# Routed experts: Gelu outputs in pairs of chunks, a lead of four chunks, and a tile's high token part on ScalarE

## The chip, the cores and the metric

The program runs on one core of one Trainium2 chip. The metric is the device time of one execution in microseconds, the median of several. The program has two parts that follow each other: an attention-like part with the shared experts (about 900 us), and the routed experts (about 510 us). Only the second is changed.

## The reference, cut to what matters

```
x = x + mlstm_cell(layernorm(x), ctx, ctx, ...)        # first part, unchanged
u = layernorm(x)
h_s = shared experts of u                              # first part, unchanged
scores = sigmoid(u @ centroids); gpk, i_topk = top_k(scores, 2); gk = gpk / scores.sum(-1)
xn = u * rsqrt(mean(u * u) + eps) * g_routed
h  = gelu(einsum('btc,ech->bteh', xn, W1_r) + b1_r)    # C 256, H 1024, 8 experts
routed = einsum('bteh,ehc->btec', h, W2_r) + b2_r
out = x + u + h_s + sum over the two chosen experts of gk * routed
```

## The kernel before, in words

The first part writes each token twice, once for each chosen expert, into a DRAM buffer sorted by expert (8 x 512 tokens, two experts each). The second part (`stage_c`, from L1034) walks over NT = 39 tiles of T = 256 sorted tokens, each with one expert. n is the tile, i = n % 2 its buffer, r = n // 2.

**Two-part products.** Each float32 factor is used as a high part (rounded to fp32r, a cast) and a low part (the factor minus its high part). A product is three matmuls: high x high, high x low, low x high. So each tile's tokens need xhi and xlo, its weights whi and wlo, and the Gelu outputs hhi and hlo.

**Tile n on TensorE** (`body`, L1141). Before the first matmul it waits for xhi, for xlo and for the first NP1 = 4 of the tile's wlo pieces (L1144 to L1146), which hold all of W1. Then it goes through M = 8 chunks m of 128 hidden units: the up-product of chunk m (six matmuls of 256 columns, L1155) into one of NU = 4 banks, and after it the second product of the chunk that lies LAG = 2 earlier (`second`, six matmuls, L1135), for m < LAG that of the tile before. Behind the up-product of chunk XSTEP = 3 come four transposes of the next tile's tokens (L1119). In the text, U3 is the moment at which the up-product of chunk 3 has been issued, U7 the same for chunk 7.

**ScalarE** (`body`, L1196), in program order for each m: Gelu of chunk m from the bank into hraw (L1206), the cast into hhi (L1209); at m = LAG the scaled output yt of the tile before (`output`, L1186, two instructions L1192); then one piece of whi (L1184, `weights`).

**VectorE** (`body`, L1264), in program order for each m: wait for hhi of the chunk, hlo = hraw - hhi (L1273), then one piece of wlo (L1233); at m = XSTEP, ahead of the piece, xT (`tokens`, L1236: two scalings out of the banks, L1242), at m = M - 2 xlo (`tokens_low`, L1247), and behind m = M - 1 four very small instructions that find the tokens' owners (`owners`).

**Which piece of weights a step makes** is decided by `piece_of` (L1079), for ScalarE and VectorE alike:

```
def piece_of(m):
    return (m - LAG) % M, m >= LAG
```

The weights of a tile are 8 pieces of 128 x 512 (4 of W1, then 4 of W2). With LAG = 2, chunks 2 to 7 of tile n make pieces 0 to 5 of tile n + 1, and chunks 0 and 1 of the next tile the pieces 6 and 7. Pieces 3 and 7 (BY_POOL, L1077) are not cast by ScalarE but by GpSimd.

**GpSimd** (`body`, L1317), in program order for each tile: the cast of piece 3 of the next tile (L1297) once the second products of the tile before are done, two indirect DMAs that add yt into the output (`add_up`, L1313) once yt is made, the cast xhi of the next tile's tokens (L1304) once xT is made, the cast of piece 7.

**SyncE** issues the loads of tile n (tokens, W1, W2, bias) once wlo of tile n - 2 is complete (L1096).

The Gelu buffers hraw, hhi and hlo have NHB = 4 slots of one chunk each.

Of the kernel before, what the change touches and what calls it, by code (L numbers as in the profile page):

```python
# [4 lines left out]
fp32 = mybir.dt.float32  # L5
# [14 lines left out]
def xattn_moe_kernel(nc, x, ctxt, ig_w, ig_b, fg_w, fg_b, ln_scale, g_s, W1_s, b1_s, W2_s, b2_s,  # L20
# [9 lines left out]
    M = HID // P  # L30
# [29 lines left out]
    with whole:  # L60
# [972 lines left out]


        stage_c = ExitStack()
        NHB = 4
        Cc = lambda name, shape, dt=fp32: sb(stage_c, name, shape, dt)
        PIECE = 2 * WN // M
        NP1 = WN // PIECE
# [45 lines left out]
        with nc.Block() as block:  # L1085
# [25 lines left out]
            @block.tensor  # L1111
            def _(pe):
                def transposes(n, i, r):
                    pe.wait_ge(t_x[i], 16 * r + 16)
                    if n > 0:
                        pe.wait_ge(t_xraw, n)
                    for k in range(KD):
                        for j in range(TJ):
                            last = nc.tensor.transpose(x_bank[k][:, j * P:(j + 1) * P], xt[i][:, j, 2 + k * P:2 + (k + 1) * P],  # L1119
                                                       ident[:, :])  # L1120
                    last.then_inc(t_tr, 1)

                def second(n, i, m):

                    pe.wait_ge(t_hhi, M * n + m + 1)
                    pe.wait_ge(t_hlo, M * n + m + 1)
                    if m % 2 == 0:
                        pe.wait_ge(t_wlo, M * n + NP1 + m // 2 + 1)
                    if m == 0 and n > 1:
                        pe.wait_ge(t_y, n - 1)  # L1130
                    h = m % NHB
                    wsl = slice(WN + m * D, WN + (m + 1) * D)
                    for j in range(TJ):
                        for t, (l, w) in enumerate(((hhi, whi), (hhi, wlo), (hlo, whi))):
                            last = nc.tensor.matmul(  # L1135
                                y_bank[i][j * D // 512][:, (j * D) % 512:(j * D) % 512 + D], l[:, h, j * P:(j + 1) * P],
                                w[i][:, wsl], start=m == 0 and t == 0 and (j * D) % 512 == 0,
                                stop=m == M - 1 and t == 2, skip_group_check=True)
                    last.then_inc(t_step, 1)

                def body(n, i, r):  # L1141
                    if n == 0:
                        transposes(0, 0, 0)
                    pe.wait_ge(t_xhi, n + 1)  # L1144
                    pe.wait_ge(t_xlo, n + 1)
                    pe.wait_ge(t_wlo, M * n + NP1)  # L1146
                    for m in range(M):

                        if not (n == 0 and m < NU):
                            pe.wait_ge(t_gelu, M * n + m - NU + 1)  # L1150
                        ub = psum[m % NU]
                        for k in range(KD):
                            wsl = slice(k * HID + m * P, k * HID + (m + 1) * P)
                            for t, (w, x_) in enumerate(((whi, xhi), (whi, xlo), (wlo, xhi))):
                                last = nc.tensor.matmul(ub[:, 0:T], w[i][:, wsl], x_[i][:, k, :],  # L1155
                                                        start=k == 0 and t == 0, stop=k == KD - 1 and t == 2)
                        last.then_inc(t_up, 1)
                        if m == XSTEP and n < NT - 1:
                            transposes(n + 1, 1 - i, r + i)
                        if m >= LAG:  # L1160
                            second(n, i, m - LAG)
                        elif n > 0:
                            second(n - 1, 1 - i, M - LAG + m)
                    if n == NT - 1:
                        for m in range(M - LAG, M):
                            second(n, i, m)
                for n in range(NT):
                    body(n, n % 2, n // 2)

            @block.scalar  # L1170
            def _(sc):
                def weights(n, i, r, m):

                    if m == 0:
                        sc.wait_ge(t_w1[i], 16 * r + 16)
                    if m == NP1:
                        sc.wait_ge(t_w2[i], 16 * r + 16)
                    if n > 1 and m == 0:

                        sc.wait_ge(t_step, M * (n - 1))  # L1180
                    if m in BY_POOL:
                        return
                    psl = slice(m * PIECE, (m + 1) * PIECE)
                    nc.scalar.copy(whi[i][:, psl], raw[i][:, psl]).then_inc(t_whi, 1)  # L1184

                def output(n, i, r):  # L1186
                    sc.wait_ge(t_step, M * n + M)
                    sc.wait_ge(t_meta, n + 1)
                    if n > 1:
                        sc.wait_ge(t_acc, 16 * TJ * (n - 1))  # L1190
                    for j in range(TJ):
                        last = nc.scalar.activation(yt[i][:, j, :], y_bank[i][j * D // 512][:, (j * D) % 512:(j * D) % 512 + D],  # L1192
                                                    ACT.Copy, scale=gate[n % NG][:, j:j + 1])
                    last.then_inc(t_y, 1)

                def body(n, i, r):  # L1196
                    if n == 0:
                        for m in range(M - LAG):
                            weights(0, 0, 0, m)
                    sc.wait_ge(t_b1[i], 16 * r + 16)  # L1200
                    for m in range(M):
                        sc.wait_ge(t_up, M * n + m + 1)
                        if not (n == 0 and m < NHB):

                            sc.wait_ge(t_step, M * n + m - NHB + 1)
                        nc.scalar.activation(hraw[:, m % NHB, :], psum[m % NU][:, 0:T], ACT.Gelu,  # L1206
                                             bias=b1[i][:, m:m + 1]).then_inc(t_gelu, 1)
                        sc.wait_ge(t_gelu, M * n + m + 1)
                        nc.scalar.copy(hhi[:, m % NHB, :], hraw[:, m % NHB, :]).then_inc(t_hhi, 1)  # L1209
                        if m == LAG and n > 0:  # L1210
                            output(n - 1, 1 - i, r - 1 + i)
                        piece, ahead = piece_of(m)
                        if not ahead:
                            weights(n, i, r, piece)
                        elif n < NT - 1:
                            weights(n + 1, 1 - i, r + i, piece)
                    if n == NT - 1:
                        output(n, i, r)
                for n in range(NT):
                    body(n, n % 2, n // 2)  # L1220

            @block.vector
            def _(dve):
# [40 lines left out]
                def body(n, i, r):  # L1264
# [4 lines left out]
                            weights(0, 0, m)  # L1269
                        owners(0, 0)  # L1270
                    for m in range(M):
                        dve.wait_ge(t_hhi, M * n + m + 1)
                        nc.vector.tensor_tensor(hlo[:, m % NHB, :], hraw[:, m % NHB, :],  # L1273
                                                hhi[:, m % NHB, :].bitcast(fp32), ALU.subtract).then_inc(t_hlo, 1)
                        piece, ahead = piece_of(m)
                        if not ahead:
                            weights(n, i, piece)
                        elif n < NT - 1:
                            if m == XSTEP:
                                tokens(n + 1, 1 - i)  # L1280
                            if m == M - 2:
                                tokens_low(n + 1, 1 - i)
                            weights(n + 1, 1 - i, piece)
                            if m == M - 1:
                                owners(n + 1, 1 - i)
                for n in range(NT):
# [3 lines left out]
            def _(pool):  # L1290
# [5 lines left out]
                    psl = slice(m * PIECE, (m + 1) * PIECE)  # L1296
                    nc.gpsimd.tensor_copy(whi[i][:, psl], raw[i][:, psl]).then_inc(t_wpool, 1)  # L1297

                def tokens(n, i):

                    if n > 1:
                        pool.wait_ge(t_up, M * (n - 1))
                    pool.wait_ge(t_xraw, n + 1)
                    nc.gpsimd.tensor_copy(xhi[i][:, :, :], xT[:, :, :]).then_inc(t_xhi, 1)  # L1304

                def add_up(n, i):

                    pool.wait_ge(t_y, n + 1)
# [7 lines left out]

                def body(n, i, r):  # L1317
                    if n == 0:
                        tokens(0, 0)
                        weights(0, 0, 0, BY_POOL[0])  # L1320
                        weights(0, 0, 0, BY_POOL[1])
                    if n < NT - 1:
# [1 line left out]
                    if n > 0:  # L1324
                        add_up(n - 1, 1 - i)
                    if n < NT - 1:
                        tokens(n + 1, 1 - i)
                        weights(n + 1, 1 - i, r + i, BY_POOL[1])
                    else:
                        add_up(n, i)  # L1330
# [28 lines left out]
```

## Time and profile before

| | |
|---|---|
| median of 3 executions | 1432.65 us (1430.29 to 1432.75) |
| the profiled execution, its own time | 1436.01 us |
| its span | 1434.3 us |
| mean granted TensorE clock over the span | 0.951 |
| routed experts, first to last TensorE matmul | 917.3 to about 1424 us |
| TensorE busy in the span | 1170.9 us (82%) |
| VectorE busy | 1026.1 us (72%) |
| ScalarE busy | 793.5 us (55%) |
| GpSimd busy | 389.5 us (27%) |

A row of the timeline gives the start in us from the span's start, the duration in us, the engine (PE is TensorE, DVE VectorE, ACT ScalarE, POOL GpSimd), the line of the kernel, the operation, output and inputs, the shape, how many instructions were merged, and in brackets the idle time of the engine just before with what ended it; "issue" means that the profile shows no releaser. A duration holds some 0.1 us in which the engine already starts its next instruction, so the distance between two starts is the better price of one of several in a row. Matmuls overlap even more: a duration of 0.28 us at a distance of 0.12 us.

### The profile page before, as it was taken

The numbers are of one execution on the slowest core, as the hardware profiler recorded it, in microseconds if no ns is written. First come the engines' busy times: TensorE is split into PE (matmuls) and PEld (weight loads), VectorE is DVE, ScalarE is ACT, GpSimd is POOL, SyncE is SP. The second block draws the span as 40 slices with busy tenths as digits, with TensorE's granted clock in tenths as the row PEclk, the third lists the DMA queues.
The fourth block names the chain that finished last, engine by engine and source line by source line (L and its number), as shares of the span: only waits on it lengthen the run. The fifth ranks groups of instructions, "written<-read, shape, count | busy, mean of one in ns | idle before, by whom it ended". The sixth has DMA issues, their size and how long they took to land. (4 is left out here: it accounts for less than half of the span.)

```text
span 1434.3 us, 22326 instructions
## 1 busy us (share of the span) xinstructions
PE 1170.9 (82%) x7861; PEld 1008.2 (70%) x7861; DVE 1026.1 (72%) x2507; ACT 793.5 (55%) x1454; POOL 389.5 (27%) x397
## 2 busy tenths in 40 slices
PE   0363698797897987997978988599999999999996
PEld 0142477576676666775766777589888999899886
DVE  2356659568567676595684654588898889888984
ACT  2101355444553554554544443488888887888785
POOL 2312122041041121221410201144334433443343
PEclk9986799999999999999999998799999999999998
DMA  4899910000010010000000000677777777777772
GB/s 125 220 265 273 288 61 30 30 30 30 30 59 30 20 41 30 30 31 30 30 15 15 31 19 27 213 206 194 194 218 210 198 190 214 216 198 194 205 220 24
DMA packets 172563, 168.08 MB, mean 117 GB/s; under 512 B 48362, under 2 KB 159860, under 8 KB 172452
## 3 DMA queue, kind: packets, MB, share of 16 engines
q1 hardware_dynamic: 120884, 109.43, 25.3%
q10 hardware_dynamic: 37264, 38.54, 10.5%
q0 software_dynamic: 14304, 18.69, 6.3%
q8 instruction: 63, 1.03, 0.3%
q14 instruction: 48, 0.39, 0.1%
HBM read 109.42 MB, written 57.22 MB: 116 GB/s over the span
## 5 line engine op out<-in xcount | busy, mean ns | idle before, releaser
L1233 DVE TENSOR_TENSOR wlo<-raw,whi 128x512 fp32r<-128x512 f32 x312 | 228.2, 732 | 35.1 <-ACT whi L1184 31.4
L1155 PE MATMUL bank<-xhi,whi 128*128 128x256 f32 x624 | 178.8, 287 | 25.5 <-issue 20.2
L1206 ACT ACTIVATE hraw<-bank,b 128x256 f32<-128x256 f32 x312 | 148.2, 475 | 86.2 <-PE bank L1155 53.1
L1273 DVE TENSOR_TENSOR hlo<-hraw,hhi 128x256 fp32r<-128x256 f32 x312 | 183.1, 587 | 17.5 <-ACT hhi L1209 5.7
L973 PE MATMUL bank<-whs,shared_hhi 128*128 128x256 f32 x512 | 150.0, 293 | 50.1 <-DVE shared_hlo L727 50.1
L1135 PE MATMUL bank<-whi,hhi 128*128 128x256 f32 x624 | 180.3, 289 | 12.8 <-issue 11.4
L523 ACT ACTIVATE shared_hraw<-bank,b1s 128x512 f32<-128x512 f32 x128 | 88.1, 688 | 180.8 <-PE bank L988 171.4
L1155 PE MATMUL bank<-xlo,whi 128*128 128x256 f32 x624 | 175.3, 281 | 0.0
L1155 PE MATMUL bank<-xhi,wlo 128*128 128x256 f32 x624 | 175.1, 281 | 0.0
L1135 PE MATMUL bank<-whi,hlo 128*128 128x256 f32 x624 | 173.4, 278 | 0.0
L1135 PE MATMUL bank<-wlo,hhi 128*128 128x256 f32 x624 | 173.3, 278 | 0.0
L727 DVE TENSOR_TENSOR shared_hlo<-shared_hraw,shared_hhi 128x512 fp32r<-128x512 f32 x128 | 89.9, 706 | 114.1 <-ACT shared_hhi L526 107.5
L458 POOL DMA_INDIRECT sorted_tokens<-rowbuf,slots x64 | 66.3, 1036 | 371.9 <-DVEq L808 354.8
L1184 ACT CAST whi<-raw 128x512 fp32r<-128x512 f32 x234 | 143.9, 616 | 17.3 <-DMA raw<-in_L_ffn_W_r_dram 17.3
L1313 POOL DMA_INDIRECT out_dram<-yt,token x78 | 121.3, 1556 | 96.1 <-ACT yt L1192 84.2
L973 PE MATMUL bank<-wls,shared_hhi 128*128 128x256 f32 x512 | 146.8, 287 | 0.0
L973 PE MATMUL bank<-whs,shared_hlo 128*128 128x256 f32 x512 | 146.5, 286 | 0.0
L973 PEld LDWEIGHTS bank<-whs,shared_hhi 128*128 128x128 f32 x512 | 100.0, 195 | 63.5 <-DVE shared_hlo L727 59.3
L1155 PEld LDWEIGHTS bank<-xhi,whi 128*128 128x128 f32 x624 | 118.4, 190 | 32.5 <-issue 32.5
L1297 POOL CAST whi<-raw 128x512 fp32r<-128x512 f32 x78 | 79.2, 1016 | 213.3 <-PE bank L1135 207.1
L1209 ACT CAST hhi<-hraw 128x256 fp32r<-128x256 f32 x312 | 126.8, 406 | 9.9
L988 PE MATMUL bank<-xhs,whs 128*128 128x512 f32 x256 | 117.4, 459 | 17.0 <-DVE xls L746 11.8
(248 smaller groups left out, 2834.7 us busy)
## 6 DMA issues: line engine op xcount, KB each, us to landing
raw<-in_L_ffn_W_r_dram SPq DMA_DIRECT2D x78, 1024.0 KB, 7.8
sorted_tokens<-base ACTq DMA_DIRECT2D x1, 33540.0 KB, 137.6
xt<-sorted_tokens SPq DMA_DIRECT2D x39, 260.0 KB
big<-in_L_ffn_W_s_dram SPq DMA_DIRECT2D x4, 1024.0 KB
xb<-in_x_dram SPq DMA_DIRECT2D x8, 512.0 KB, 4.6
cb<-in_ctx_dram SPq DMA_DIRECT2D x8, 512.0 KB, 3.6
xr<-in_x_dram SPq DMA_DIRECT2D x8, 512.0 KB, 3.6
out_dram<-base ACTq DMA_DIRECT2D x8, 512.0 KB, 2.9
```

What stands on the lines that cost most here:

```text
L523: nc.scalar.activation(hraw[:, k % NHB, :], up_bank[k % 2][:, :], ACT.Gelu, bias=b1s[:, k // M, k % M:k % M + 1]).then_inc(gelu_done, 1)
L727: tt(hlo[:, k % NHB, :], hraw[:, k % NHB, :], hhi[:, k % NHB, :].bitcast(fp32), ALU.subtract).then_inc(hlo_ready, 1)
L973: last = mm(down_bank[j // 2][:, (j % 2) * D:(j % 2 + 1) * D], h[:, k % NHB, j * P:(j + 1) * P], w[:, e, wsl], start=k == 0 and t == 0 and ...
L988: last = mm(up_bank[k % 2][:, :], w[:, e, wsl], x_[:, c, :], start=c == 0 and t == 0, stop=c == KD - 1 and t == 2)
L1135: last = nc.tensor.matmul(y_bank[i][j * D // 512][:, (j * D) % 512:(j * D) % 512 + D], l[:, h, j * P:(j + 1) * P], w[i][:, wsl], start=m = ...
L1155: last = nc.tensor.matmul(ub[:, 0:T], w[i][:, wsl], x_[i][:, k, :], start=k == 0 and t == 0, stop=k == KD - 1 and t == 2)
L1184: nc.scalar.copy(whi[i][:, psl], raw[i][:, psl]).then_inc(t_whi, 1)
L1206: nc.scalar.activation(hraw[:, m % NHB, :], psum[m % NU][:, 0:T], ACT.Gelu, bias=b1[i][:, m:m + 1]).then_inc(t_gelu, 1)
L1209: nc.scalar.copy(hhi[:, m % NHB, :], hraw[:, m % NHB, :]).then_inc(t_hhi, 1)
L1233: nc.vector.tensor_tensor(wlo[i][:, psl], raw[i][:, psl], whi[i][:, psl].bitcast(fp32), ALU.subtract).then_inc(t_wlo, 1)
L1273: nc.vector.tensor_tensor(hlo[:, m % NHB, :], hraw[:, m % NHB, :], hhi[:, m % NHB, :].bitcast(fp32), ALU.subtract).then_inc(t_hlo, 1)
L1313: nc.gpsimd.indirect_dma_start(out=out_r, out_offset=bass.IndirectOffsetOnAxis(ap=token[n % NG][:, j:j + 1], axis=0), in_=yt[i][:, j, :], ...
```

## The change

What it does: the Gelu buffers get NHB = 8 slots, and LAG becomes 4, for the second products and for `piece_of` alike. The cast hhi and the subtraction hlo are made for two chunks at once, at odd m, as 128 x 512. TensorE waits for them at even m. The cast xhi moves from GpSimd to ScalarE, to m = LAG = 4, ahead of the output of the tile before. On VectorE, xT and xlo stand behind the step's piece of wlo in place of ahead of it.

```diff
--- before.py
+++ after.py
@@ -1033,7 +1033,8 @@
 
 
         stage_c = ExitStack()
-        NHB = 4
+        NHB = 8
+        LAG = 4
         Cc = lambda name, shape, dt=fp32: sb(stage_c, name, shape, dt)
         PIECE = 2 * WN // M
         NP1 = WN // PIECE
@@ -1122,9 +1123,9 @@
 
                 def second(n, i, m):
 
-                    pe.wait_ge(t_hhi, M * n + m + 1)
-                    pe.wait_ge(t_hlo, M * n + m + 1)
                     if m % 2 == 0:
+                        pe.wait_ge(t_hhi, (M * n + m) // 2 + 1)
+                        pe.wait_ge(t_hlo, (M * n + m) // 2 + 1)
                         pe.wait_ge(t_wlo, M * n + NP1 + m // 2 + 1)
                     if m == 0 and n > 1:
                         pe.wait_ge(t_y, n - 1)
@@ -1183,6 +1184,10 @@
                     psl = slice(m * PIECE, (m + 1) * PIECE)
                     nc.scalar.copy(whi[i][:, psl], raw[i][:, psl]).then_inc(t_whi, 1)
 
+                def tokens(n, i):
+                    sc.wait_ge(t_xraw, n + 1)
+                    nc.scalar.copy(xhi[i][:, :, :], xT[:, :, :]).then_inc(t_xhi, 1)
+
                 def output(n, i, r):
                     sc.wait_ge(t_step, M * n + M)
                     sc.wait_ge(t_meta, n + 1)
@@ -1195,6 +1200,7 @@
 
                 def body(n, i, r):
                     if n == 0:
+                        tokens(0, 0)
                         for m in range(M - LAG):
                             weights(0, 0, 0, m)
                     sc.wait_ge(t_b1[i], 16 * r + 16)
@@ -1205,8 +1211,12 @@
                             sc.wait_ge(t_step, M * n + m - NHB + 1)
                         nc.scalar.activation(hraw[:, m % NHB, :], psum[m % NU][:, 0:T], ACT.Gelu,
                                              bias=b1[i][:, m:m + 1]).then_inc(t_gelu, 1)
-                        sc.wait_ge(t_gelu, M * n + m + 1)
-                        nc.scalar.copy(hhi[:, m % NHB, :], hraw[:, m % NHB, :]).then_inc(t_hhi, 1)
+                        if m % 2:
+                            h = m % NHB
+                            sc.wait_ge(t_gelu, M * n + m + 1)
+                            nc.scalar.copy(hhi[:, h - 1:h + 1, :], hraw[:, h - 1:h + 1, :]).then_inc(t_hhi, 1)
+                        if m == LAG and n < NT - 1:
+                            tokens(n + 1, 1 - i)
                         if m == LAG and n > 0:
                             output(n - 1, 1 - i, r - 1 + i)
                         piece, ahead = piece_of(m)
@@ -1269,18 +1279,21 @@
                             weights(0, 0, m)
                         owners(0, 0)
                     for m in range(M):
-                        dve.wait_ge(t_hhi, M * n + m + 1)
-                        nc.vector.tensor_tensor(hlo[:, m % NHB, :], hraw[:, m % NHB, :],
-                                                hhi[:, m % NHB, :].bitcast(fp32), ALU.subtract).then_inc(t_hlo, 1)
+                        if m % 2:
+                            h = m % NHB
+                            dve.wait_ge(t_hhi, (M * n + m) // 2 + 1)
+                            nc.vector.tensor_tensor(hlo[:, h - 1:h + 1, :], hraw[:, h - 1:h + 1, :],
+                                                    hhi[:, h - 1:h + 1, :].bitcast(fp32), ALU.subtract).then_inc(t_hlo, 1)
                         piece, ahead = piece_of(m)
                         if not ahead:
                             weights(n, i, piece)
                         elif n < NT - 1:
+                            weights(n + 1, 1 - i, piece)
+                        if n < NT - 1:
                             if m == XSTEP:
                                 tokens(n + 1, 1 - i)
                             if m == M - 2:
                                 tokens_low(n + 1, 1 - i)
-                            weights(n + 1, 1 - i, piece)
                             if m == M - 1:
                                 owners(n + 1, 1 - i)
                 for n in range(NT):
@@ -1295,13 +1308,6 @@
                         pool.wait_ge(t_step, M * (n - 1))
                     psl = slice(m * PIECE, (m + 1) * PIECE)
                     nc.gpsimd.tensor_copy(whi[i][:, psl], raw[i][:, psl]).then_inc(t_wpool, 1)
-
-                def tokens(n, i):
-
-                    if n > 1:
-                        pool.wait_ge(t_up, M * (n - 1))
-                    pool.wait_ge(t_xraw, n + 1)
-                    nc.gpsimd.tensor_copy(xhi[i][:, :, :], xT[:, :, :]).then_inc(t_xhi, 1)
 
                 def add_up(n, i):
 
@@ -1316,7 +1322,6 @@
 
                 def body(n, i, r):
                     if n == 0:
-                        tokens(0, 0)
                         weights(0, 0, 0, BY_POOL[0])
                         weights(0, 0, 0, BY_POOL[1])
                     if n < NT - 1:
@@ -1324,7 +1329,6 @@
                     if n > 0:
                         add_up(n - 1, 1 - i)
                     if n < NT - 1:
-                        tokens(n + 1, 1 - i)
                         weights(n + 1, 1 - i, r + i, BY_POOL[1])
                     else:
                         add_up(n, i)
```

## Rows read from the trace of the kernel before

**Rows 1.** Windows: stretch, width, busy us of PE, PEld, DVE, ACT, POOL, granted clock, DMA, GB/s.

```profile
1150.00:1200.00 50.00, 46.76 (x387) 45.59 (x388) 44.81 (x89) 40.79 (x95) 20.78 (x20) 1.00 0.74 202
```

**Rows 2.** Waits from 930 to 1415 us: us in total, times, the longest.

```profile
PE bank L1155 <- issue: 20.2, 37, 0.6
...
PE bank L1135 <- issue: 11.4, 30, 0.6
```

**Rows 3.** Timeline of TensorE through one tile.

```profile
1181.17 0.60 PE L1119 MATMUL bank<-ident,xt 128*128 128x128 f32 x4
...
1186.34 0.36 PE L1135 MATMUL bank<-whi,hhi 128*128 128x256 f32 x1 [0.39 <-issue]
...
1189.23 0.36 PE L1155 MATMUL bank<-xhi,whi 128*128 128x256 f32 x1 [0.53 <-issue]
...
1192.80 0.28 PE L1135 MATMUL bank<-whi,hhi 128*128 128x256 f32 x1
...
1194.19 0.60 PE L1119 MATMUL bank<-ident,xt 128*128 128x128 f32 x4
1194.55 0.36 PE L1135 MATMUL bank<-whi,hhi 128*128 128x256 f32 x1
...
1195.34 0.28 PE L1155 MATMUL bank<-xhi,whi 128*128 128x256 f32 x1
```

**Rows 4.** Timeline of ScalarE in the same tile.

```profile
1193.00 0.48 ACT L1206 ACTIVATE hraw<-bank,b 128x256 f32<-128x256 f32 x1 [0.49 <-PE bank L1155]
1193.51 0.41 ACT L1209 CAST hhi<-hraw 128x256 fp32r<-128x256 f32 x1
1193.82 0.84 ACT L1192 ACTIVATE yt<-bank,gate 128x256 f32<-128x256 f32 x2
1194.55 0.62 ACT L1184 CAST whi<-raw 128x512 fp32r<-128x512 f32 x1
```

**Rows 5.** Timeline of VectorE in the same tile.

```profile
1188.45 0.68 DVE L1247 TENSOR_TENSOR xlo<-xT,xhi 128x512 fp32r<-128x512 f32 x1
...
1192.55 0.75 DVE L1273 TENSOR_TENSOR hlo<-hraw,hhi 128x256 fp32r<-128x256 f32 x1
...
1193.95 0.43 DVE L1273 TENSOR_TENSOR hlo<-hraw,hhi 128x256 fp32r<-128x256 f32 x1
...
1196.35 0.87 DVE L1242 TENSOR_SCALAR xT<-bank,gr_col 128x256 f32<-128x256 f32 x2
1197.14 0.68 DVE L1233 TENSOR_TENSOR wlo<-raw,whi 128x512 fp32r<-128x512 f32 x1
1197.74 1.53 DVE L1273 TENSOR_TENSOR hlo<-hraw,hhi 128x256 fp32r<-128x256 f32 x1
1199.19 1.08 DVE L1233 TENSOR_TENSOR wlo<-raw,whi 128x512 fp32r<-128x512 f32 x1
```

**Rows 6.** Timeline of GpSimd in the same tile.

```profile
1192.40 0.62 POOL L1297 CAST whi<-raw 128x512 fp32r<-128x512 f32 x1 [5.71 <-PE bank L1135]
...
1197.79 1.19 POOL L1304 CAST xhi<-xT 128x512 fp32r<-128x512 f32 x1
1198.35 1.36 POOL L1297 CAST whi<-raw 128x512 fp32r<-128x512 f32 x1
```

**Rows 7.** Page: DMA issues, with the median us from issue to landing.

```profile
raw<-in_L_ffn_W_r_dram SPq DMA_DIRECT2D x78, 1024.0 KB, 7.8
```

**Rows 8.** Timeline of TensorE: the first matmul behind an idle stretch.

```profile
279.29 0.46 PE L946 MATMUL bank<-vaug,chunk 128*128 128x99 f32 x2 [2.25 <-DVE chunk L662]
...
843.27 0.79 PE L988 MATMUL bank<-xhs,whs 128*128 128x512 f32 x1 [4.51 <-DVE xls L746]
```

**Rows 9.** Windows as in rows 1, behind idle stretches.

```profile
279.30:284.00 4.70, 4.70 (x35) 4.38 (x35) 3.15 (x12) 1.19 (x2) 0.00 (x0) 1.00 0.00 0
843.30:848.70 5.40, 5.40 (x13) 4.24 (x14) 0.69 (x1) 2.41 (x3) 0.00 (x0) 0.50 0.00 0
917.30:920.40 3.10, 3.08 (x14) 3.10 (x15) 2.18 (x7) 2.47 (x6) 0.62 (x1) 0.50 1.02 392
```

## The prediction

> **What bounds the kernel now.** I read the windows of the routed part first, then its waits, then the timelines of one tile side by side. The granted clock is 1.00 there, and in 50 us TensorE is busy for 46.8, VectorE for 44.8, ScalarE for 40.8 and GpSimd for 20.8 [rows 1]. No engine is full all the time: TensorE leads, and the others are near enough to hold it up through waits. The waits say where. Ahead of the up-products (L1155) TensorE stood idle 37 times, 20.2 us in total, ahead of the second products (L1135) 30 times, 11.4 us [rows 2]: the same two places in every tile. The timeline shows them. A tile lasts from the transposes at 1181.17 to those at 1194.19, 13.02 us [rows 3]. The first idle time ends at 1186.34, where a second product waited for an hlo that GpSimd's casts had held up. The second ends at 1189.23, the first up-product of the next tile, 0.10 us behind the end of xlo (1188.45 + 0.68) [rows 3, 5]. So the handover from tile to tile already lies on the path: what VectorE finishes last for the next tile starts TensorE's next tile.
>
> **The change, part by part.** Times below are us after U3. One step (up-product and second product) takes 1194.19 - 1192.80 = 1.39, half of it 0.70. The up-product of chunk 4 starts 1195.34 - 1194.19 = 1.15 after U3 [rows 3], so U7 lies at 1.15 + 0.70 + 3 x 1.39 = 6.02, and the second product behind it, the last work of the tile, is issued by 6.72.
>
> *Lead of four.* `piece_of` now gives pieces 0 to 3 of the next tile to chunks 4 to 7 (before: to chunks 2 to 5). TensorE still starts a tile only when all four are there (L1146). Piece 3 of wlo now stands on VectorE behind the pair hlo of chunks 6 and 7, which needs the Gelu of chunk 7, so the last up-product of the tile. Before, the last thing asked for was xlo, two chunks earlier. This is the step that decides.
>
> *The token part on ScalarE.* xhi waits for xT, which VectorE now makes behind the pair hlo of chunks 2 and 3 and behind piece 7. ScalarE stands still in program order meanwhile, and behind it are queued yt, three pieces of whi and the Gelus of chunks 5, 6 and 7.
>
> *Prices.* A Gelu starts 0.20 after the up-product is issued (1192.80, 1193.00), the dependent cast 0.51 after it [rows 3, 4]. A ScalarE instruction with no such wait starts its duration less 0.10 after the one before: 0.52 behind a 128 x 512 cast of 0.62, 0.38 behind a Gelu of 0.48; yt takes 0.73 (1193.82 to 1194.55) [rows 4]. The pair hhi and xhi have the form of the whi cast, so 0.62 each. hlo starts 0.03 behind hhi's end (1193.51 + 0.41, 1193.95) [rows 4, 5]. A 128 x 512 subtraction lasts 0.68 and the next starts 0.60 after it (1197.14, 1197.74), xT lasts 0.87 [rows 5]; the pair hlo has the form of wlo.
>
> *The chain.* Gelu 3 at 0.20; pair hhi 0.71; pair hlo 0.71 + 0.62 + 0.03 = 1.36; wlo 7 at 1.96; xT 2.56 to 3.43; xhi 3.46. ScalarE could have begun xhi right behind Gelu 4, at 1.85 + 0.20 + 0.38 = 2.43, so it loses 1.03. Then yt 3.98, whi 0 4.71, Gelu 5 5.23, pair hhi 5.74, whi 1 6.26, Gelu 6 6.78, whi 2 7.16, Gelu 7 7.68, pair hhi 8.19, done 8.81. VectorE: wlo 2 at 7.16 + 0.62 + 0.03 = 7.81, xlo 8.41, pair hlo 9.01 (hhi would allow 8.84), wlo 3 9.61, done 10.29. TensorE starts the next tile at 10.39, and from there to the next U3 takes 1194.19 - 1189.23 = 4.96 [rows 3]. Period: 10.39 + 4.96 = 15.35 against 13.02.
>
> *GpSimd against VectorE.* The casts of pieces 3 and 7 stay. The first starts 1.00 after the last second product of the tile before (that one at 1192.80 - 1.39 = 1191.41, the cast at 1192.40), which is now U3 + 0.36 [rows 3, 6]: 1.36, just where the pair hlo starts. The second takes the place of the xhi cast, 3.97 behind yt's start (1193.82, 1197.79) [rows 4, 6]: 3.98 + 3.97 = 7.95, beside wlo 2. Both lie on the chain. What such a meeting costs: a lone cast made hlo 0.75 in place of 0.43, so 0.32; the two in a row cost 1.53 - 0.43 and 1.08 - 0.68, 1.50 for two, 0.75 each [rows 5, 6]. In that costlier case hlo had started just ahead of the cast, as here, so I take a value nearer to it, 0.60 each: 1.20, ends 0 and 1.50. Period 16.55. VectorE's hlo (1197.74) began 0.05 ahead of the cast (1197.79) and was held up all the same. The Trainium skill, SBUF — State Buffer, on the port pair that VectorE and GpSimd share, says that whichever instruction starts first keeps it and the other blocks; by that rule both casts would wait for VectorE and the 1.20 would fall away. The row speaks against it.
>
> *The clock.* TensorE is now idle from 6.72 + 0.16 to 11.59, 4.7 us in each tile. Behind an idle stretch of 4.51 the clock was 0.50 for 5.4 us, behind one of 2.25 it stayed at 1.00 [rows 8, 9]. 4.7 is nearest to 4.51, so I take it that every tile starts at 1.2 GHz. The price lies between 3.10 us at half speed (the first tile), 1.55 lost, and 5.40 us, 2.70 lost [rows 9]; the middle is 2.1, wholly on the path, as the 4.96 us up to U3 are TensorE's own work. Period 18.65.
>
> *Edits with no price.* The saving by pairs (four instructions less on ScalarE, 4 x (2 x 0.31 - 0.52) = 0.4 us a tile, as much on VectorE) lies in engines that now wait. The eight slots never bind: the chunk eight earlier is long consumed. SyncE's loads are released by piece 7 two steps later and needed two steps later; they land in 7.8 us [rows 7], inside one period. The last tile has four second products behind its last up-product in place of two, the same work in all. The first tile makes its xhi on ScalarE in 0.62 and starts as before.
>
> *Sum.* 39 tiles have 38 handovers. 38 x (18.65 - 13.02) = 214. The profiled execution took 1436.0, so 1650; it lies 3.4 above the median of the runs, so **1647**.
>
> **The rivals.**
>
> *The clock holds.* Work lies closely around the stall, and no row has this rhythm of 12 busy and 4.7 idle. Then the period is 16.55, 38 x 3.53 = 134, and the time 1567. Against it: 4.51 was enough.
>
> *VectorE is not held up.* If the casts wait, the period is 15.35 + 2.1 = 17.45, 38 x 4.43 = 168, the time 1601. The idle stretch would still be 3.5. Against it stand both rows of held-up hlo [rows 5].
>
> *Faster: the late piece is there in time.* Without the xhi cast in GpSimd's queue and with four steps of lead no second product waits for hlo, and if the tile could start without waiting, all idle time of the waits goes, 20.2 + 11.4 = 31.6 us [rows 2], and the time is 1401. It decides whether wlo 3 is done by 6.72. My chain has it at 10.29 before any meeting, and even with no lateness of ScalarE it would need 6.02 + 0.20 + 0.51 + 0.65 + 0.60 + 0.68 = 8.66. So I would have to misread the order of the program.
>
> **How the numbers follow.** The forecast (clock down, meetings paid) has 0.66, the clock that holds 0.15, VectorE not held up 0.14, the faster case 0.05, of which I give 0.03 to faster and 0.01 to each of the other two, for a handover eased only in part. A measurement tells about 0.2% from no change. The bounds of the forecast's terms are 15.35 + 1.55 = 16.90 (1580) and 15.35 + 1.50 + 2.70 = 19.55 (1681). The range reaches from the first rival to a little above the upper bound, 1567 to 1685; it leaves out the faster case and what errors in the rows could add.
>
> **What the profile would show.** Right: in each tile one idle stretch of TensorE of 3.5 to 5 us, ahead of L1155, ended by wlo; none ahead of L1135; ScalarE idle for about 1 us ahead of xhi; Gelu 7 more than 1 us behind its up-product; the clock at 0.50 in part of every tile; a distance between transposes of 17 to 19.5 us. Wrong would be: a distance near 16.5 with the clock at 1.00; hlo and wlo at 0.68 beside the casts; or no stall at L1155, which would end the whole argument.

## The result, and the profile after

The changed kernel takes 1653.2 us in the median of 4 executions (1650.5 to 1655.4), the kernel before in the same comparison 1432.7 (1430.3 to 1434.6): a ratio of 1.154, 95% interval 1.152 to 1.156. The forecast was 1647, slower, with a range of 1567 to 1685.

In the windows of the routed part (columns as in rows 1) TensorE fell from 46.8 busy us in 50 to 34.7, and the granted clock from 1.00 to 0.86, against [rows 1]:

```profile
1150.00:1200.00 50.00, 34.67 (x252) 34.15 (x251) 29.54 (x51) 27.58 (x57) 14.63 (x11) 0.86 0.57 156
```

The waits of the changed kernel, 930 to 1630 us (total, times, longest), answer to [rows 2]:

```profile
PE bank L1156 <- DVE wlo L1243: 193.1, 38, 5.2
DVE wlo L1243 <- ACT whi L1185: 172.4, 93, 2.5
...
DVE hlo L1285 <- ACT hhi L1217: 104.0, 111, 2.0
ACT xhi L1189 <- DVE xT L1252: 50.8, 37, 1.4
```

The 20.2 us ahead of the up-products have become 193.1, about 5.1 us in each of the 38 handovers, and wlo ends them. Ahead of the second products TensorE no longer waits at all. ScalarE stands still for 1.4 us ahead of each xhi. TensorE's timeline, against [rows 3] (the lines have moved by one: L1120 are the transposes, L1156 the up-products, L1136 the second products):

```profile
1200.87 0.60 PE L1120 MATMUL bank<-ident,xt 128*128 128x128 f32 x4
...
1212.86 0.55 PE L1156 MATMUL bank<-xhi,whi 128*128 128x256 f32 x1 [5.10 <-DVE wlo L1243]
...
1220.16 0.60 PE L1120 MATMUL bank<-ident,xt 128*128 128x128 f32 x4
...
1226.78 0.28 PE L1136 MATMUL bank<-whi,hlo 128*128 128x256 f32 x1
1232.15 0.55 PE L1156 MATMUL bank<-xhi,whi 128*128 128x256 f32 x1 [5.09 <-DVE wlo L1243]
...
1238.42 0.60 PE L1120 MATMUL bank<-ident,xt 128*128 128x128 f32 x4
```

The last second product of the tile starts 6.62 us after U3 (1226.78), as forecast (issued by 6.72); then TensorE stands still until its restart, the first up-product of the next tile. From one set of transposes to the next it is 19.29 us, then 18.26. All tiles but the first few alternate like this, 18.77 in the mean, where the kernel before had 13.02; why they alternate, no run here shows. From the transposes to the restart it is 11.99 both times. What alternates is the way from the restart to the next transposes: 7.30, then 6.27, where the kernel before needed 4.96. The window behind the first restart shows why this way is longer: TensorE works at half its clock, 1.2 GHz. The granted clock is 0.50 in the first 2 us behind each of the 38 restarts.

```profile
1212.90:1217.90 5.00, 5.00 (x23) 5.00 (x24) 0.90 (x3) 1.77 (x4) 0.00 (x0) 0.50 0.35 39
```

The chain that I had written down, on ScalarE, in the tile that begins at 1200.87 ([rows 4] before):

```profile
1202.91 0.47 ACT L1212 ACTIVATE hraw<-bank,b 128x256 f32<-128x256 f32 x1 [0.71 <-PE bank L1156]
1204.76 0.62 ACT L1189 CAST xhi<-xT 128x512 fp32r<-128x512 f32 x1 [1.37 <-DVE xT L1252]
1205.28 0.84 ACT L1197 ACTIVATE yt<-bank,gate 128x256 f32<-128x256 f32 x2
...
1208.96 0.47 ACT L1212 ACTIVATE hraw<-bank,b 128x256 f32<-128x256 f32 x1
1209.46 0.62 ACT L1217 CAST hhi<-hraw 128x512 fp32r<-128x512 f32 x1
```

and on VectorE and GpSimd ([rows 5, 6] before):

```profile
1202.23 0.69 DVE L1285 TENSOR_TENSOR hlo<-hraw,hhi 128x512 fp32r<-128x512 f32 x1 [0.70 <-ACT hhi L1217]
1202.84 1.10 DVE L1243 TENSOR_TENSOR wlo<-raw,whi 128x512 fp32r<-128x512 f32 x1
1203.86 0.86 DVE L1252 TENSOR_SCALAR xT<-bank,gr_col 128x256 f32<-128x256 f32 x2
...
1209.09 1.31 DVE L1243 TENSOR_TENSOR wlo<-raw,whi 128x512 fp32r<-128x512 f32 x1
1210.32 1.08 DVE L1257 TENSOR_TENSOR xlo<-xT,xhi 128x512 fp32r<-128x512 f32 x1
1211.33 0.68 DVE L1285 TENSOR_TENSOR hlo<-hraw,hhi 128x512 fp32r<-128x512 f32 x1
1211.93 0.68 DVE L1243 TENSOR_TENSOR wlo<-raw,whi 128x512 fp32r<-128x512 f32 x1
```

```profile
1202.32 1.08 POOL L1310 CAST whi<-raw 128x512 fp32r<-128x512 f32 x1 [9.74 <-PE bank L1136]
...
1208.26 1.54 POOL L1319 DMA_INDIRECT out_dram<-yt,token  x1 [0.31 <-issue]
1209.25 1.60 POOL L1310 CAST whi<-raw 128x512 fp32r<-128x512 f32 x1
```

ScalarE waits 1.37 us for xT. The last Gelu starts 8.09 after U3 (forecast without meetings 7.68). Piece 3 of wlo stands last and frees TensorE at 1212.86. Around GpSimd's two casts VectorE's subtractions last longer than their 0.68 us: wlo 7 behind the pair hlo 1.10, wlo 2 1.31, xlo 1.08.

### The profile page after: what moved, and what is told of

Its sections match the earlier page's. It is cut to its first block and busy times, and to the rows that moved or that the text cites. A ratio compares the mean times of both kernels' runs of the same rounds, so it can differ in the third digit from the quotient of the medians.

```text
span 1653.6 us, 21817 instructions
## 1 busy us (share of the span) xinstructions
PE 1230.6 (74%) x7861; PEld 1074.1 (65%) x7861; DVE 1004.6 (61%) x2351; ACT 787.9 (48%) x1337; POOL 390.4 (24%) x358
## 5 line engine op out<-in xcount | busy, mean ns | idle before, releaser
L1243 DVE TENSOR_TENSOR wlo<-raw,whi 128x512 fp32r<-128x512 f32 x312 | 252.2, 809 | 182.1 <-ACT whi L1185 176.2
L1156 PE MATMUL bank<-xhi,whi 128*128 128x256 f32 x624 | 198.6, 318 | 198.4 <-DVE wlo L1243 198.4
L1156 PEld LDWEIGHTS bank<-xhi,whi 128*128 128x128 f32 x624 | 136.6, 219 | 205.3 <-issue 205.3
L1310 POOL CAST whi<-raw 128x512 fp32r<-128x512 f32 x78 | 102.7, 1317 | 435.7 <-PE bank L1136 383.7
L1136 PE MATMUL bank<-whi,hhi 128*128 128x256 f32 x624 | 192.7, 309 | 0.0
L1156 PE MATMUL bank<-xlo,whi 128*128 128x256 f32 x624 | 191.4, 307 | 0.0
L1156 PE MATMUL bank<-xhi,wlo 128*128 128x256 f32 x624 | 191.1, 306 | 0.0
L1136 PE MATMUL bank<-wlo,hhi 128*128 128x256 f32 x624 | 188.6, 302 | 0.0
L1136 PE MATMUL bank<-whi,hlo 128*128 128x256 f32 x624 | 187.0, 300 | 0.0
L1285 DVE TENSOR_TENSOR hlo<-hraw,hhi 128x512 fp32r<-128x512 f32 x156 | 108.1, 693 | 111.8 <-ACT hhi L1217 111.8
L1156 PEld LDWEIGHTS bank<-xlo,whi 128*128 128x128 f32 x624 | 136.5, 219 | 0.0
L1156 PEld LDWEIGHTS bank<-xhi,wlo 128*128 128x128 f32 x624 | 134.8, 216 | 0.0
```

Source lines behind the costliest of these rows:

```text
L1136: last = nc.tensor.matmul(y_bank[i][j * D // 512][:, (j * D) % 512:(j * D) % 512 + D], l[:, h, j * P:(j + 1) * P], w[i][:, wsl], start=m = ...
L1243: nc.vector.tensor_tensor(wlo[i][:, psl], raw[i][:, psl], whi[i][:, psl].bitcast(fp32), ALU.subtract).then_inc(t_wlo, 1)
L1285: nc.vector.tensor_tensor(hlo[:, h - 1:h + 1, :], hraw[:, h - 1:h + 1, :], hhi[:, h - 1:h + 1, :].bitcast(fp32), ALU.subtract).then_inc(t_ ...
```

## The experiments

Ten kernels ran. I compare ratios to the kernel before in the same comparison, since its median moved between 1432 and 1437; one hundredth of the ratio is 14.3 us.

**a1_fill: TensorE kept busy in the stall.** The results of the filling matmuls are read by nobody; the rest is the changed kernel.

```diff
                             second(n, i, m - LAG)
+                            if m == M - 1 and n < NT - 1:
+                                pe.wait_ge(t_xraw, n + 2)
+                                for f in range(24):
+                                    nc.tensor.matmul(x_bank[1][:, T:2 * T], whi[i][:, 0:P], xhi[i][:, 0, :],
+                                                     start=True, stop=True)
```

> The changed kernel with 24 matmuls more per tile, whose results nobody reads, behind the last second product of a tile, into a free half bank: some 2.8 us of TensorE work inside the 5.1 us in which it stood idle. My theory (the idle stretch itself lasts as long as the chain on ScalarE and VectorE; on top of it the clock falls in it and takes about 1.8 us per tile): the chain is as long as before, 11.99 us from U3 to the restart in the changed kernel's trace, but the tile starts at full clock, so the period is 11.99 + 4.96 = 16.95 in place of 18.77 us, 38 x 1.82 = 69 us less than the changed kernel: about 1584 us, granted clock 1.00 in the stage. Rival (the first steps of a tile are slow for another reason, such as late Gelus or banks): no faster than 1653 us.

Measured: 1592.4 us, ratio 1.109 (1.105 to 1.113), 64 us less than the changed kernel for 24 matmuls more per tile. TensorE's timeline of this kernel:

```profile
1196.93 0.60 PE L1120 MATMUL bank<-ident,xt 128*128 128x128 f32 x4
...
1203.67 2.89 PE L1166 MATMUL bank<-xhi,whi 128*128 128x256 f32 x24
1208.92 0.36 PE L1156 MATMUL bank<-xhi,whi 128*128 128x256 f32 x1 [2.36 <-DVE wlo L1248]
...
1213.88 0.60 PE L1120 MATMUL bank<-ident,xt 128*128 128x128 f32 x4
```

The window from this restart to the next transposes:

```profile
1208.90:1213.88 4.98, 4.96 (x42) 4.98 (x43) 2.28 (x6) 3.48 (x7) 0.00 (x0) 1.00 0.37 45
```

The chain is 11.99 to the hundredth; the next transposes come at 1213.88, 4.96 after the restart, with the clock at 1.00. So most tiles last 16.96, and the clock accounts for the difference. The forecast was 69 us less. The 5 us between are nearly covered by three periods that are still longer by 1.4 to 1.6 us each, 4.4 together (their granted clock was 0.50 in the first 2 us behind the restart).

**a2_xhi_pool: the cast xhi back on GpSimd.**

```diff
-                        if m == LAG and n < NT - 1:
-                            tokens(n + 1, 1 - i)
...
+                        tokens(n + 1, 1 - i)
                         weights(n + 1, 1 - i, r + i, BY_POOL[1])
```

The removed lines are ScalarE's, the added one is GpSimd's, behind `add_up`.

> The changed kernel with only the cast xhi back on GpSimd, ahead of its cast of piece 7. My theory (ScalarE stands in program order until xT is there, and everything behind it comes late): ScalarE no longer waits, Gelu 7 starts about 1.4 us earlier, GpSimd's two casts in a row meet VectorE once more; restart of TensorE at about U3 + 9.7 in place of 12.0, idle stretch about 3 us, period 14.7 to 15.2 us if the clock holds: 1500 to 1520 us; 1575 us if it falls. Rival (only the place of wlo piece 3 behind the last pair counts, and ScalarE's wait is hidden): the chain from Gelu 7 on is unchanged, and one more cast meets VectorE: 1650 us or more.

Measured: 1588.6 us, ratio 1.109 (1.106 to 1.113), 64 us less than the changed kernel. The direction is mine, the size is not: I had named 1575 us for a clock that falls, and put the restart at U3 + 9.7, where it came at 10.59. VectorE's timeline shows what I had priced too low, the two casts in a row:

```profile
1210.52 2.69 DVE L1236 TENSOR_TENSOR wlo<-raw,whi 128x512 fp32r<-128x512 f32 x2
1213.13 1.08 DVE L1250 TENSOR_TENSOR xlo<-xT,xhi 128x512 fp32r<-128x512 f32 x1
```

That is 1.41 and 0.40 us over the undisturbed 1.28 and 0.68. The idle stretch was 3.70 us, and behind it too the clock fell: a period of 17.07 against 10.59 + 4.96 = 15.55.

**a3_wlo3_first: piece 3 of wlo ahead of the last pair hlo.**

```diff
                     for m in range(M):
+                        if m == M - 1 and n < NT - 1:
+                            weights(n + 1, 1 - i, piece_of(m)[0])
                         if m % 2:
...
-                        elif n < NT - 1:
+                        elif n < NT - 1 and m < M - 1:
                             weights(n + 1, 1 - i, piece)
```

> The changed kernel with VectorE's two last instructions of a tile exchanged: piece 3 of wlo ahead of the pair hlo of chunks 6 and 7. My theory: VectorE is full from wlo 1 to wlo 3 in the changed kernel, so only the pair's own 0.60 us leave the path to the restart: 38 x 0.6 = 23 us less, about 1630 us, and the idle stretch is still over 4 us with the clock falling. Rival (the dependence of piece 3 on the last Gelu is the whole loss): the stall goes almost wholly and the time is under 1500 us.

Measured: 1631.3 us, ratio 1.139 (1.135 to 1.142), 22 us less, as expected; the restart comes at U3 + 11.39 in place of 11.99. That piece 3 depends on the last Gelu through program order is real but small; VectorE's own queue is nearly as late.

**a4_lead2: the pieces' lead back at two steps.**

```diff
         LAG = 4
+        LEAD = 2
...
-            return (m - LAG) % M, m >= LAG
+            return (m - LEAD) % M, m >= LEAD
...
-                    if n > 1 and m == 0:
+                    if n > 1 and m == NP1:
                         sc.wait_ge(t_step, M * (n - 1))
...
```

> The changed kernel, but with the lead of the weights' pieces back at two steps, while the second products keep their lead of four (ScalarE's wait for the second products of the tile before stands at piece 4 in place of piece 0, so that the early pieces are not held up). xlo stays at step 6. My theory: all four wlo pieces of W1 are there at step 5, the last thing asked for is xlo behind wlo 4, at about U3 + 8.6 plus one meeting with a GpSimd cast; period 13.6 to 14.4 us with the clock at 1.00: 1455 to 1490 us. Rival (the move of xhi to ScalarE makes the loss, not the pieces): over 1600 us.

Measured: 1588.4 us, ratio 1.108 (1.105 to 1.111), 66 us less than the changed kernel. A miss: I had expected 1455 to 1490, and the rival over 1600. VectorE's timeline of this kernel, in the tile whose transposes start at 1207.84:

```profile
1214.65 0.69 DVE L1286 TENSOR_TENSOR hlo<-hraw,hhi 128x512 fp32r<-128x512 f32 x1 [0.33 <-ACT hhi L1218]
1215.26 2.10 DVE L1244 TENSOR_TENSOR wlo<-raw,whi 128x512 fp32r<-128x512 f32 x2
1217.28 1.08 DVE L1258 TENSOR_TENSOR xlo<-xT,xhi 128x512 fp32r<-128x512 f32 x1
```

The pieces of W1 are in time, but xlo took their place as the last thing: behind the pair hlo of 4 and 5 stand two pieces and xlo, and the second cast of GpSimd meets the second piece and xlo. The restart came at 10.63, ended by xlo. I had counted one meeting of 0.6 us, it was 0.43 ahead of xT, then 2.10 for two pieces in place of 1.28, and 1.08 for xlo in place of 0.68. Behind the idle stretch of 3.73 us the clock was then down (0.50 for the first 2 us), which I had excluded. A lead of two alone is not the cure as long as ScalarE and xlo stay late. What it is worth with the clock held, no run shows.

**a8_fill_xT_first: xT ahead of the pair, with the clock held.** The edit is on top of a1_fill, so that only the chain speaks.

```diff
                     for m in range(M):
+                        if m == XSTEP and n < NT - 1:
+                            tokens(n + 1, 1 - i)
                         if m % 2:
...
-                            if m == XSTEP:
-                                tokens(n + 1, 1 - i)
```

> The kernel with the filling matmuls (a1_fill, which keeps the clock at 1.00, so that the chain alone sets the time), and in addition VectorE makes xT at the start of step 3, ahead of the pair hlo and piece 7. My theory (ScalarE loses 1.4 us per tile in front of the cast xhi, and all of it is on the path): ScalarE's wait goes, the chain from U3 to the restart falls from 11.99 to about 10.6 us, 38 x 1.4 = 53 us less than a1_fill: about 1540 us. Rival (VectorE is the longer branch, as it is full from piece 1 to piece 3, so ScalarE's wait is mostly covered): under 15 us less, 1577 us or more.

Measured: 1527.5 us, ratio 1.067 (1.065 to 1.069), 60 us less than a1_fill. ScalarE's timeline beside TensorE's:

```profile
1210.93 0.48 ACT L1217 ACTIVATE hraw<-bank,b 128x256 f32<-128x256 f32 x1 [0.71 <-PE bank L1156]
1211.31 0.61 ACT L1194 CAST xhi<-xT 128x512 fp32r<-128x512 f32 x1
```

```profile
1208.89 0.60 PE L1120 MATMUL bank<-ident,xt 128*128 128x128 f32 x4
1219.40 0.36 PE L1156 MATMUL bank<-xhi,whi 128*128 128x256 f32 x1 [0.88 <-DVE wlo L1248]
```

On VectorE, in the same tile:

```profile
1209.53 0.88 DVE L1257 TENSOR_SCALAR xT<-bank,gr_col 128x256 f32<-128x256 f32 x2
...
1210.92 1.10 DVE L1248 TENSOR_TENSOR wlo<-raw,whi 128x512 fp32r<-128x512 f32 x1
```

The wait of 1.37 ahead of xhi is gone and the restart comes at 10.51: 1.48 less, 56 us in 38 handovers (the rest of the 60 are the three slow periods of a1_fill). The edit takes more than ScalarE's wait off the path: wlo 7 is still held up to 1.10 by GpSimd's first cast, but xT stands ahead of it now. No other single edit shortened the way from U3 to the restart by more: a2_xhi_pool by 1.40, a4_lead2 by 1.36, a3_wlo3_first by 0.60. These shares overlap, and they do not add up.

**a6_casts_early and a9_fill_casts_early: GpSimd's casts away from VectorE's full stretch**, first on the changed kernel, then with the clock held.

```diff
-                        pool.wait_ge(t_step, M * (n - 1))
+                        pool.wait_ge(t_up if m < NP1 else t_step, M * (n - 1))
...
                         weights(n + 1, 1 - i, r + i, BY_POOL[0])
+                        weights(n + 1, 1 - i, r + i, BY_POOL[1])
                     if n > 0:
                         add_up(n - 1, 1 - i)
-                    if n < NT - 1:
-                        weights(n + 1, 1 - i, r + i, BY_POOL[1])
-                    else:
+                    if n == NT - 1:
                         add_up(n, i)
```

> The changed kernel, but GpSimd casts piece 3 as soon as the up-products that read its place are done (at the start of a tile, where VectorE is idle), and piece 7 where piece 3 was, ahead of the output DMAs. My theory (each cast that meets VectorE holds it up): the meeting beside wlo 2 and xlo, 0.82 + 0.40 us in the changed kernel's trace, goes; the restart comes at U3 + 10.8 in place of 12.0, 38 x 1.2 = 46 us less, and the shorter idle stretch of 3.9 us leaves the clock's cost as it is or lowers it a little: 1590 to 1607 us. Rival (VectorE keeps what it started first, the casts give way): no change, 1653 us.

> The kernel with the filling matmuls (a1_fill, clock at 1.00) and GpSimd's two casts earlier, as in a6_casts_early. That run came out at 1629 us where I had expected 1590 to 1607, although its restart came at U3 + 10.98 in place of 11.99. My theory: the meeting of wlo 2 and xlo with a GpSimd cast costs the chain 1.0 us per tile, and in a6_casts_early the clock took back what the chain gave. With the clock held, the whole 1.0 shows: 38 x 1.0 = 38 us less than a1_fill, about 1553 us, restart at U3 + 11.0. Rival (the early casts cost something else, such as a load of the weights that comes too late for GpSimd): 10 us less at most, 1580 us or more.

Measured: 1629.4 us, ratio 1.138 (1.136 to 1.140), for the first, 23 us less than the changed kernel and a miss (1590 to 1607 was expected); 1559.5, ratio 1.084 (1.081 to 1.087), for the second, 36 us less than a1_fill. VectorE's timeline of the second:

```profile
1206.65 1.49 DVE L1248 TENSOR_TENSOR wlo<-raw,whi 128x512 fp32r<-128x512 f32 x2
1208.05 0.68 DVE L1262 TENSOR_TENSOR xlo<-xT,xhi 128x512 fp32r<-128x512 f32 x1
```

xlo is back at 0.68, and the two pieces last 1.49 with the 0.2 us in which they wait for ScalarE. The meeting was a real cost. In this tile (transposes at 1199.22) the restart came at 1210.20, 10.98 after U3; in the next at 1226.56, 11.40 after 1215.16. In both, GpSimd's cast of piece 3 waits for its load. In the first it then comes too late to touch the chain (U3 + 10.25), in the second it comes at U3 + 9.19 and holds up the pair hlo of chunks 6 and 7, to 1.10:

```profile
1224.35 0.81 POOL L1314 CAST whi<-raw 128x512 fp32r<-128x512 f32 x1 [0.25 <-DMA raw<-in_L_ffn_W_r_dram]
1224.60 1.10 DVE L1290 TENSOR_TENSOR hlo<-hraw,hhi 128x512 fp32r<-128x512 f32 x1
```

So the rival has a part, and it accounts for most of the first miss. The 10.98 from which I had argued was one tile of a6_casts_early. From its fourth tile on the restart comes between 10.97 and 11.58, 11.29 in the mean, because the late cast meets VectorE in many tiles; in 19 tiles it waits for its load (us in total, times, the longest):

```profile
POOL whi L1309 <- DMA raw<-in_L_ffn_W_r_dram: 20.6, 19, 2.6
```

Taken over these tiles, a6_casts_early shortens the chain by 0.70 us and the period by 0.63 (18.77 to 18.14), a9_fill_casts_early by 0.80 and 0.75 (17.05 to 16.30). So my theory that the clock had taken back what the chain gave holds for 0.07 us of 0.70 only. The rest of the distance between 23 and 36 us is the better restart of the second kernel and the spread of the ratios, some 7 us for the 36.

**a5_lead2_xlo4 and a7_xT_first: the causes taken out together.** Both have the edit of a4_lead2 and xlo at step 4; a7_xT_first has xT at the start of step 3 besides.

```diff
-                            if m == M - 2:
+                            if m == LAG:
                                 tokens_low(n + 1, 1 - i)
```

> All three causes taken out, pairs and the lead of four of the second products kept: the weights' pieces with a lead of two, xT at the start of step 3, xlo at step 4. Chain by rows of the changed kernel: xT 0.95 to 1.8 us after U3, xhi 2.43, whi 2 3.68, pair hhi 4.71, wlo 2 4.33, xlo 4.93, pair hlo 5.53, wlo 3 6.13 to 6.81, restart 6.91 against 6.72 without any stall; plus 0.4 at most for a meeting. Period 11.8 to 12.3 us, clock at 1.00: 1390 to 1410 us, faster than both kernels. Rival (the pairs with their late hhi and the xhi cast on ScalarE are a loss by themselves): over 1433 us.

> The kernel a7_xT_first (1397 us) with xT back behind the pair hlo and piece 7 or 1 of step 3, as in the change; lead of two for the pieces and xlo at step 4 kept. My theory (the late xT makes ScalarE stand, and all behind it is late): pair hlo 45 at U3 + 6.8, behind xlo 6.98, wlo 3 7.58 to 8.26, restart 8.36 against 6.91, idle stretch 1.5 us, clock at 1.00, period 13.3: 38 x 1.3 = 49 us more than a7_xT_first, 1438 to 1455 us. Rival (with the pieces' lead of two the place of xT costs nothing): 1405 us or less.

Measured: a7_xT_first 1396.6 us, ratio 0.976 (0.974 to 0.978), faster than both kernels and inside its forecast; a5_lead2_xlo4 1456.8, ratio 1.013 (1.011 to 1.016), 54 us more for the place of xT alone where 49 was expected, with the restart at U3 + 8.54 and the clock at 1.00. The window and a handover of a7_xT_first:

```profile
1150.00:1200.00 50.00, 49.34 (x418) 48.64 (x418) 44.96 (x80) 43.52 (x89) 23.44 (x18) 1.00 0.79 226
```

```profile
1205.90 0.60 PE L1121 MATMUL bank<-ident,xt 128*128 128x128 f32 x4
1212.96 0.36 PE L1157 MATMUL bank<-xhi,whi 128*128 128x256 f32 x1 [0.17 <-issue]
1217.92 0.60 PE L1121 MATMUL bank<-ident,xt 128*128 128x128 f32 x4
```

The restart is at U3 + 7.06, the period 12.02, TensorE is busy for 49.3 of 50 us. Pairs, eight slots, a lead of four for the second products and xhi on ScalarE are all in it. Together they need not cost anything. What each is worth alone, no run shows, except for the move of xhi in the next experiment.

**b1_xhi_only: the kernel before with the xhi move alone**, behind the cast hhi of chunk 4, VectorE's order untouched.

> The kernel before with only the cast xhi moved to ScalarE (behind the cast hhi of chunk 4), the rest as it was: single chunks, lead of two, xT ahead of the piece. My theory: the move itself is no loss; GpSimd's two casts in a row, which hold up hlo 4 and the piece behind it by 1.5 us, become one, so the idle time ahead of the second products (11.4 us in all) goes and the one ahead of the up-products shrinks: 1405 to 1425 us. Rival (ScalarE is too full to take one cast more per tile): 1433 us or more.

Measured: 1417.0 us, ratio 0.990 (0.987 to 0.992). In the kernel before, where xT stands ahead of the piece, the same move is a small gain of 15 us, inside its forecast. A new small wait remained, of a second product for hhi, because ScalarE is now the late one:

```profile
1211.16 0.36 PE L1135 MATMUL bank<-whi,hhi 128*128 128x256 f32 x1 [0.36 <-ACT hhi L1214]
```

## Why the prediction was right

**The lead of the pieces.** Right: piece 3 of wlo ends the stall in all 38 handovers. By itself the pair ahead of it is worth 22 us (a3_wlo3_first). But a lead of two alone left 1588 us (a4_lead2): it had to come together with xlo at step 4 (a5_lead2_xlo4, 1457) and xT at the start of step 3 (a7_xT_first, 1397).

**ScalarE's wait for xT.** Forecast 1.03 us from start to start. Counted the same way it is 3.89 - 2.42 = 1.47 (the row shows 1.37 of it as idle), which is the 1.03 and the 0.43 by which the first meeting made xT late. Taking both away is worth 1.48 per tile on the path (a8_fill_xT_first).

**The chain.** Forecast without meetings 10.39 to the restart. The measured 11.99 is that, plus 0.43 where the first cast of GpSimd held up wlo 7 (xT at 2.99 in place of 2.56), plus 0.61 by which xlo started late (9.45 in place of 8.41 + 0.43), plus 0.41 by which it held up the pair hlo, plus 0.15 for the restart itself, which came 0.25 us behind wlo's end (1211.93 + 0.68, 1212.86) and not 0.10. The 0.10 was read behind an xlo, and behind an xlo it holds again in a4_lead2 (1217.28 + 1.08, restart 1218.47). So the meetings cost 1.45 on the path. I had taken 1.20, with 1.50 as the upper end: mis-sized, because I counted one instruction held up by 0.60 for each cast, where the first cast cost 0.43 and the second held up two instructions.

**The clock.** Forecast 2.1 us per tile, measured 18.77 - 16.95 = 1.82, alternating 2.34 and 1.31 (7.30 and 6.27 against 4.96). The forecast's 2.1 was the middle between two half-speed stretches elsewhere in the program (3.10 and 5.40 us), so that it came near is partly luck. a1_fill shows the cause by itself: 64 us over 38 handovers, 1.7 each. The Trainium skill, TensorE: Matmul & The Clock Gate, section HAM oscillation, describes a kernel in which every group of matmuls starts cold behind its wait. The trace agrees, with a clock of 0.50 behind each restart here.

**The sum.** 18.65 forecast, 18.77 measured. It fits this closely by luck, because two errors nearly cancel: 0.40 too little in the chain, 0.28 too much for the clock. The period accounts for the whole loss: 38 x (18.77 - 13.02) = 218.5 us, and the spans of the two profiled executions differ by 219.3.

**The rivals.** The clock that holds would have given 1567 by my sum; held by hand it gave 1592. VectorE not held up: the longer subtractions around each cast speak against it, and a9_fill_casts_early shows them shorter once the cast is away. The first meeting does look like the rule that I had cited from the Trainium skill, SBUF — State Buffer (section Who interferes with whom): the pair hlo, 0.09 us ahead of the cast (1202.23, 1202.32), kept its 0.69, and the cast took 1.08. But the rule's loser only changes place. The cast then held up the next subtraction, wlo 7, by 0.42, and that is on the chain too. In the second meeting the trace doesn't agree with the rule: wlo 2 started 0.16 us ahead of the cast (1209.09, 1209.25) and took 1.31 all the same. The traces point at GpSimd's indirect DMA instruction. In the changed kernel 37 second casts began 0.54 to 0.58 us before that instruction's row ended, and the subtraction under way was longer by 0.60 to 0.70 us in every one; the 37 first casts have no such instruction ahead, and there it never was. In a9_fill_casts_early, where 27 casts met a subtraction under way and none began more than 0.04 us before the DMA's row ended, none of these subtractions was longer either. The place in the tile changed along with the order, so this is a pattern and not a shown cause. The faster case did not come for this kernel, yet a7_xT_first, which meets its condition (the wlo pieces are there almost when the tile's work ends), came to 1397, near its 1401. It is another kernel, with three more edits, so this confirms the condition and not the forecast of that rival.

**Edits with no price.** Nothing speaks against them: the eight slots and the last tile show no wait behind its restart, no cast of the changed kernel waits for a load, and TensorE waits no more ahead of the second products. What the pairs save by themselves no run measured.

## What to carry to other kernels

When the lead of one stage is changed, look at every other queue that is steered by the same number, and ask which instruction is now the last one that the next tile needs; write its chain down through each engine's program order. An engine that waits in order for one small operand delays all that is queued behind it, so put the producer of that operand first. An idle stretch of TensorE that recurs in every tile can cost twice, for itself and for the half clock behind it, so hold the clock in one experiment before pricing the chain. A restart read in one tile may not be the mean: look at all tiles before explaining a miss by it.

## What was not expected of the hardware

Recurring idle stretches of 3.70 us (a2_xhi_pool) and 3.73 us (a4_lead2) were followed by the half clock just as those of 5.1 were; those of 2.36 us (a1_fill) and 1.64 us (a5_lead2_xlo4) were not, but for a few tiles of a1_fill. From the restart to the next transposes, 4.96 us at full clock, it took 6.78 us in the mean behind 5.1 us of idle, 6.80 behind 4.5 (a3_wlo3_first), 6.48 and 6.45 behind 3.7, 5.06 behind 2.36. In the kernel before, the shortest stretch followed by the half clock that I had listed was 4.51 us. And the two kernels of 3.7 us, built differently, share the same period of 17.07 us in nearly every tile.

GpSimd's cast, 0.62 us in rows 6, lasted 1.08 in its first meeting with VectorE's subtractions and 1.60 in its second, while VectorE lost 0.42 and 1.03 us: both engines lose, and together more than the cast is long.
